# Placing the transposed maxima ahead of the parts' store on SyncE's queue

## The chip, the cores and the metric

The kernel runs on one core of one Trainium2 chip. The metric is the device time of one execution in microseconds (us); less is better. The core has TensorE (PE, matmuls), VectorE (DVE), ScalarE (ACT), GpSimd (POOL) and SyncE (SP), which here issues nearly all DMA transfers. Each engine runs its own program in order, and semaphores tie them together.

## The reference

Four layers on x of shape (32, 256, 128), each with a residual and a layer norm behind it: an attention with low-rank terms on q and v, a mixture of experts, a causal attention with rotary positions, and a routed spline network. What matters here is in the two attentions:

```
q, k, v = heads(x @ w_qkv)                 # 16 heads of 8, 256 positions, 32 sequences
att = softmax(q @ k.T * scale, axis=-1)    # second attention: causal
y = (att @ v).reshape(B, T, C) @ w_proj
x = layernorm(x + y)
```

## The kernel before

`attention` is built twice, as `attn0` and `attn1` (causal, rotary). One step of its pipeline takes in one sequence (a block); five steps lie between a block's load and its layer norm, and each engine runs `step` with the blocks at their lags: `st.has(2)` is the block that came in two steps ago. Three slots of `q_st` and `k_st` hold the stacks of three blocks. 5 steps are written out, then a loop runs three steps in a turn, then the rest is written out.

The scores need more than bf16, so GpSimd splits q and k of the entering block into three bf16 parts (L260 to L270, the last one counted by `lo_kept`). SyncE stores `parts` to a scratch in DRAM with two transfers (L218 and L220, counted by `parts_stored`) and one step later loads six stacks from it into `q_st` and `k_st` (L204): 72 rows a head, in which a single bf16 matmul sums the products of the parts.

The scores are made twice. `score_rows` (L523 is the causal mask, L527 the matmul) puts queries on the partitions; VectorE takes the row maxima (L346), splits them in two bf16 values (L357, L359, `mparts`), PE transposes these (L463) and ScalarE copies them to `mT_sb`, in two halves of 8 heads: half 0 with L331 at the twelfth of 16 score pairs of the step, half 1 with L302 early in the next step. A DMA of 8 KB, the placing, puts each half in two more rows of `q_st`: L225 for half 0, L193 for half 1. `score_cols` (L545 is the mask, L549 the matmul) then makes the scores again with keys on the partitions and the maximum already taken off; it waits for `m_placed[0]` at its first head of a step, for `m_placed[1]` at its ninth. ScalarE takes the exponential (L290), and PE sums the values (L566).

PE's step is written out by hand: 16 times a column score, a row score and whatever the table `AT` sets behind that pair, such as the transposition of x (L450), q and k (L471) and v (L493). SyncE's step has this order: the load of x for the next block (L184); wait for `mT_kept`, placing of half 1 (L193); wait for `parts_stored` and the six stack loads (L204); in `attn0` a load of `x_all` (L208); wait for `lo_kept` and for the scratch slot's former readers, and the two stores (L218, L220); wait for `mT_kept`, placing of half 0 (L225). GpSimd waits for `parts_stored` of the block before, before it writes `parts` again. ScalarE waits for the placing before it writes the same half of `mT_sb` again.

Of the kernel before, what the change touches and what calls it, by code (L numbers as in the profile page):

```python
# [26 lines left out]
KROWS = PARTS * PARTS * D  # L27
MROWS = 2
K_BLOCK = PARTS
STORES, STACKS = 2, PARTS  # L30
NH = H // 2
# [39 lines left out]
def apart(eng, mem):  # L71

    eng.sem_inc(mem["apart"], 1)


def wait(eng, sem, value):

    if not isinstance(value, int) or value > 0:
        eng.wait_ge(sem, value)


def pipeline(eng, step, slots=SLOTS, depth=DEPTH, total=B, ahead=1):


    first = depth
    loops = (total - ahead - first) // slots
    for s in range(first):
        step(Step(0, s, slots, total))
    with eng.Fori(0, loops) as i:
        for r in range(slots):  # L90
            step(Step(i, first + r, slots, total))
    for s in range(first + slots * loops, total + depth - 1):
        step(Step(0, s, slots, total))


def attention(nc, name, mem, causal, x_dram, lora, rope):
# [12 lines left out]
    with ExitStack() as ctx:  # L109
        def sb(label, shape, dt=F32):  # L110
            return ctx.enter_context(nc.sbuf_tensor(f"{name}_{label}", shape, dt))

        def sem(label):
            return nc.alloc_semaphore(name=f"{name}_{label}")

        scratch = nc.dram_tensor(f"{name}_scratch", (SLOTS, K_BLOCK + 2 * PARTS - 1, P, N), BF16, kind="Internal").ap()
        x_in, q_st, k_st, v_sb = (mem[k] for k in ("x_in", "q_st", "k_st", "v_sb"))
# [7 lines left out]
        mT_sb = sb("mT_sb", [MROWS * NH, 2, N], BF16)  # L125
# [25 lines left out]
        m_placed = [[sem(f"m_placed{g}{j}") for j in range(SLOTS)] for g in range(2)]  # L151
# [5 lines left out]
        xT_kept, qk_kept, v_kept, max_kept, mhi_kept, mparts_kept, mT_kept, probs_kept, oT_kept = (  # L157
            sem(x) for x in ("xT_kept", "qk_kept", "v_kept", "max_kept", "mhi_kept", "mparts_kept", "mT_kept",
                             "probs_kept", "oT_kept"))
# [17 lines left out]
        @block.sync  # L177
        def _(sp):
            def load_x(st, lag):

                wait(sp, xT_ready, st.seq(lag, c=1 - SLOTS))
                src = x_all[:, bass.ds(st.seq(lag, TB), TB), :] if x_dram is None else \
                    x_dram[:, bass.ds(st.seq(lag, TB), TB), :]
                sp.dma_start(x_in[:, st.slot(lag), :, :], src).then_inc(x_loaded[st.slot(lag)], 16)  # L184

            def step(st):
                if st.has(-1) and (x_dram is None or st.loop or st.off >= AHEAD - 1):
                    load_x(st, -1)
                if st.has(3):

                    sp.wait_ge(mT_kept, st.seq(3, 2, 2))
                    sl = st.slot(3)
                    sp.dma_start(q_st[KROWS:KROWS + MROWS, sl, NH:H, :], mT_sb[:, 1, :]).then_inc(m_placed[1][sl], 16)  # L193
                if st.has(1):
                    sl = st.slot(1)
                    sp.wait_ge(parts_stored[sl], st.turn(1, 16 * STORES))
                    apart(sp, mem)

                    wait(sp, cols_ready, st.seq(SLOTS + 1, H, H))

                    for j in range(PARTS):
                        rows = slice(PARTS * D * j, PARTS * D * (j + 1))
                        for stack, block, stacked in ((q_st, 0, q_stacked), (k_st, K_BLOCK + j, k_stacked)):
                            sp.dma_start(stack[rows, sl, :, :].rearrange("p h n -> p (h n)"),  # L204
                                         scratch[sl, block:block + PARTS].rearrange("a (d h) n -> (a d) (h n)", d=D))\
                                .then_inc(stacked[sl], 16)
                if st.has(2) and x_dram is not None:
                    sp.dma_start(x_all[:, bass.ds(st.seq(2, TB), TB), :],  # L208
                                 x_dram[:, bass.ds(st.seq(2, TB), TB), :]).then_inc(x_old_loaded[st.slot(2)], 16)
                if st.has(0):  # L210
                    sl = st.slot(0)
                    sp.wait_ge(lo_kept, st.seq(0, c=1))
                    apart(sp, mem)

                    wait(sp, q_stacked[sl], st.turn(SLOTS, 16 * STACKS))
                    apart(sp, mem)
                    wait(sp, k_stacked[sl], st.turn(SLOTS, 16 * STACKS))
                    sp.dma_start(scratch[sl, 0:2 * PARTS].rearrange("b p n -> p b n"),  # L218
                                 parts[:, :, :, :].rearrange("p s j n -> p (s j) n")).then_inc(parts_stored[sl], 16)
                    sp.dma_start(scratch[sl, 2 * PARTS:K_BLOCK + 2 * PARTS - 1].rearrange("b p n -> p b n"),  # L220
                                 parts[:, 1, 0:PARTS - 1, :]).then_inc(parts_stored[sl], 16)
                if st.has(2):
                    sp.wait_ge(mT_kept, st.seq(2, 2, 1))
                    sl = st.slot(2)
                    sp.dma_start(q_st[KROWS:KROWS + MROWS, sl, 0:NH, :], mT_sb[:, 0, :]).then_inc(m_placed[0][sl], 16)  # L225

            if x_dram is None:
                load_x(Step(0, 0, SLOTS, B), 0)
            pipeline(sp, step)

        @block.gpsimd
# [1595 lines left out]
```

## Time and profile before

| | us |
|---|---|
| median of 3 runs | 1456.69 (1455.31 to 1460.36) |
| profiled execution | 1455.56 |
| its span | 1453.8 |
| PE busy in the span | 1117.4 (77%) |
| DVE / ACT / POOL busy | 1095.9 / 841.6 / 540.3 |

The first attention lies at about 35 to 535 us of the span, the mixture of experts behind it, the second attention at about 606 to 1180, and the spline network takes the rest. A row of the views below names line, engine, operation and tiles; in a timeline the first number is the start in us from the start of the span, the second the duration, and a bracket at the end gives the time for which the engine was idle before and what ended it. Ends of matmuls are modelled.

### The profile page before, as it was taken

What the parts mean: (1) busy time and instruction counts of PE and PEld (TensorE: products, weight loads), DVE (VectorE), ACT (ScalarE), POOL (GpSimd) and SP (SyncE); (2) the same over time, 40 slices, a digit from 0 to 9 for tenths busy, and PEclk for the clock granted to TensorE, in tenths of its full rate; (3) what the DMA queues carried; (4) which work ended last, traced back from release to release, by engine and by line L of the source; (5) the groups of instructions that cost most, each with busy time, mean ns of one, the idle gap of its engine ahead of it and who ended that gap; (6) DMA issues with size and microseconds to landing.
All of it is one profiled execution on the core that took longest, in us unless ns stands there. A gap on an engine that the chain in (4) does not pass through costs nothing. (4 is left out here: it accounts for less than half of the span.)

```text
span 1453.8 us, 36143 instructions
## 1 busy us (share of the span) xinstructions
PE 1117.4 (77%) x11411; PEld 778.6 (54%) x11411; DVE 1095.9 (75%) x2949; ACT 841.6 (58%) x1840; POOL 540.3 (37%) x568
## 2 busy tenths in 40 slices
PE   2699999999999995139999999999999948103220
PEld 1466666666666653126777777777777724002120
DVE  4589999999999976526677676676776756898996
ACT  1277777777777763616666666666666635103554
POOL 5323233332332203154455444554444142003555
PEclk9899999999999998559999999999999978655555
DMA  1655556556465513044444444444444202000111
GB/s 45 151 124 134 137 120 140 126 128 140 116 138 133 116 29 122 11 120 103 115 114 113 108 115 105 116 115 104 119 103 115 67 16 101 0 0 0 30 36 51
DMA packets 122513, 137.26 MB, mean 94 GB/s; under 512 B 12560, under 2 KB 110160, under 8 KB 113232
## 3 DMA queue, kind: packets, MB, share of 16 engines
q1 hardware_dynamic: 121408, 136.45, 38.8%
q8 instruction: 34, 0.56, 0.2%
q14 instruction: 31, 0.25, 0.1%
q10 hardware_dynamic: 1040, 0.00, 0.0%
HBM read 85.03 MB, written 37.75 MB: 84 GB/s over the span
## 5 line engine op out<-in xcount | busy, mean ns | idle before, releaser
L346 DVE TENSOR_REDUCE attn_negmax<-attn_row_ps 128x2 f32<-128x512 f32 (+1 forms) x1024 | 606.5, 618 | 216.0 <-PE attn_row_ps L527 203.6
L290 ACT ACTIVATE attn_probs<-attn_col_ps 128x512 f32<-128x512 f32 (+1 forms) x1024 | 539.9, 547 | 238.0 <-PE attn_col_ps L549 221.3
L527 PE MATMUL attn_row_ps<-k_st,q_st 72*128 72x256 bf16 (+1 forms) x2048 | 368.0, 261 | 15.3 <-DMA k_st<-attn_scratch 13.9
L549 PE MATMUL attn_col_ps<-q_st,k_st 74*128 74x256 bf16 (+1 forms) x2048 | 368.7, 261 | 2.7 <-ACT attn_probs L290 1.0
L566 PE MATMUL attn_out_ps<-attn_probs,v_sb 128*32 128x256 f32 (+1 forms) x4096 | 247.3, 359 | 1.3 <-ACT attn_probs L290 1.3
L549 PEld LDWEIGHTS attn_col_ps<-q_st,k_st 74*128 74x128 bf16 x2048 | 179.4, 98 | 91.6 <-ACT attn_probs L290 32.3
L527 PEld LDWEIGHTS attn_row_ps<-k_st,q_st 72*128 72x128 bf16 x2048 | 201.1, 99 | 40.7 <-issue 15.3
L275 POOL TENSOR_TENSOR attn_rstd<-attn_var,minus_half 128x2 f32<-128x2 f32 x64 | 45.5, 711 | 384.2 <-DVE attn_var L410 384.2
L523 PE MATMUL attn_row_ps<-mask_qk,ident_h 128*128 128x256 bf16 x512 | 140.8, 275 | 18.4 <-DMA k_st<-attn_scratch 17.8
L566 PEld LDWEIGHTS attn_out_ps<-attn_probs,v_sb 128*32 128x32 f32 x4096 | 106.9, 109 | 86.2 <-issue 20.4
L545 PE MATMUL attn_col_ps<-mask_kq,ident_h 128*128 128x256 bf16 x512 | 141.5, 276 | 13.8 <-DMA q_st<-attn_mT_sb 11.6
L250 POOL TENSOR_TENSOR attn_q_half<-attn_q_half,sin 128x512 f32<-128x512 f32 x32 | 40.6, 1267 | 182.5 <-ACT attn_qk L317 182.5
L1516 POOL TENSOR_TENSOR ffn_rstd<-ffn_var,minus_half 128x8 f32<-128x8 f32 x19 | 31.9, 1680 | 167.7 <-DVE ffn_var L1538 167.7
L260 POOL TENSOR_SCALAR attn_parts<-attn_qk 128x512 bf16<-128x512 f32 x64 | 39.7, 620 | 124.5 <-ACT attn_qk L314 112.8
L471 PE MATMUL attn_in_ps<-attn_xT,wqk 128*128 128x256 f32 x256 | 79.5, 437 | 2.4 <-ACT attn_xT L296 2.4
L1460 PE MATMUL ffn_r_ps<-ffn_table_hm,ffn_ohT 128*128 128x193 bf16 x64 | 21.0, 361 | 74.4 <-ACT ffn_ohT L1472 74.4
L545 PEld LDWEIGHTS attn_col_ps<-mask_kq,ident_h 128*128 128x128 bf16 x512 | 49.5, 97 | 50.6 <-issue 18.3
L263 POOL TENSOR_TENSOR attn_rest<-attn_qk,attn_parts 128x512 f32<-128x512 f32 x64 | 74.1, 1157 | 5.3
L270 POOL TENSOR_TENSOR attn_parts<-attn_rest,attn_parts 128x512 bf16<-128x512 f32 x64 | 74.0, 1157 | 5.3
L1449 PE MATMUL ffn_o_ps<-ident_h,ffn_onehot 128*128 128x128 bf16 x64 | 10.1, 312 | 73.4 <-PEq L1164 73.4
L523 PEld LDWEIGHTS attn_row_ps<-mask_qk,ident_h 128*128 128x128 bf16 x512 | 49.3, 96 | 28.1 <-issue 18.5
L1479 ACT ACTIVATE ffn_z<-ffn_y,ffn_shift,ffn_rstd 128x128 f32<-128x128 f32 x64 | 26.4, 482 | 54.9 <-DVE ffn_shift L1543 54.9
(228 smaller groups left out, 1687.2 us busy)
## 6 DMA issues: line engine op xcount, KB each, us to landing
q_st<-attn_scratch SPq DMA_DIRECT2D x192, 192.0 KB
k_st<-attn_scratch SPq DMA_DIRECT2D x192, 192.0 KB
attn_scratch<-attn_parts SPq DMA_DIRECT2D x64, 384.0 KB, 3.0
attn_scratch<-attn_parts SPq DMA_DIRECT2D x64, 128.0 KB, 3.7
x_in<-in_L_attn_x_dram SPq DMA_DIRECT2D x32, 128.0 KB, 2.1
x_all<-in_L_attn_x_dram SPq DMA_DIRECT2D x32, 128.0 KB, 7.0
moe_xs<-x_all SPq DMA_DIRECT2D x8, 512.0 KB, 3.0
x_in<-x_mid SPq DMA_DIRECT2D x32, 128.0 KB, 2.1
```

The lines of the kernel that those rows point to most:

```text
L250: nc.gpsimd.tensor_tensor(q_half[:, :, :], q_half[:, :, :], sin, ALU.mult).then_inc(sin_done, 1)
L263: nc.gpsimd.tensor_tensor(rest[:, :, :], qk[:, :, :], parts[:, :, 0, :], ALU.subtract)\
L270: nc.gpsimd.tensor_tensor(parts[:, :, 2, :], rest[:, :, :], parts[:, :, 1, :], ALU.subtract)\
L275: nc.gpsimd.tensor_tensor(rstd[:, :], var[:, :], mem["minus_half"][:, 0:TB], ALU.pow)\
L290: nc.scalar.activation(probs[:, u % 2, j, 0:W], col_ps[:, n % 2, 0:W], ACT.Exp, scale=scale).then_inc(probs_kept, 1)
L346: nc.vector.tensor_reduce(negmax[:, t, 2 * p:2 * p + 2], row_ps[:, row_bank(st, u), 0:2 * keys].rearrange("p (a k) -> p a k", a=2), AX_X, ...
L471: last = nc.tensor.matmul(in_ps[:, s * N:(s + 1) * N], wqk[:, s, :], xT[:, st.slot(0), :], start=True, stop=True)
L523: nc.tensor.matmul(seen[:, :, keys - P:keys], ident_h[:, :], mask_qk[:, :, :], start=True, stop=False, skip_group_check=True)
L527: last = nc.tensor.matmul(bank[:, a * keys:(a + 1) * keys], q_st[0:KROWS, sl, h, t * P:(t + 1) * P], k_st[0:KROWS, sl, h, 0:keys], start=n ...
L545: nc.tensor.matmul(seen[:, :, 0:P], ident_h[:, :], mask_kq[:, :, :], start=True, stop=False, skip_group_check=True)
L549: last = nc.tensor.matmul(bank[:, t * N:(t + 1) * N - first], k_st[0:rows, sl, h, t * P:(t + 1) * P], q_st[0:rows, sl, h, first:N], start= ...
L566: last = nc.tensor.matmul(out_ps[32 * j:32 * j + 32, g * N + first:(g + 1) * N], v_sb[:, st.slot(lag), t, 32 * h:32 * h + 32], probs[:, u ...
```

## The change

In SyncE's step the wait for the first half of the transposed maxima and its placing stand ahead of the wait for the parts and their two stores, in place of behind them. Nothing else is changed; both attentions use this code.

```diff
@@ -207,6 +207,10 @@
                 if st.has(2) and x_dram is not None:
                     sp.dma_start(x_all[:, bass.ds(st.seq(2, TB), TB), :],
                                  x_dram[:, bass.ds(st.seq(2, TB), TB), :]).then_inc(x_old_loaded[st.slot(2)], 16)
+                if st.has(2):
+                    sp.wait_ge(mT_kept, st.seq(2, 2, 1))
+                    sl = st.slot(2)
+                    sp.dma_start(q_st[KROWS:KROWS + MROWS, sl, 0:NH, :], mT_sb[:, 0, :]).then_inc(m_placed[0][sl], 16)
                 if st.has(0):
                     sl = st.slot(0)
                     sp.wait_ge(lo_kept, st.seq(0, c=1))
@@ -219,10 +223,6 @@
                                  parts[:, :, :, :].rearrange("p s j n -> p (s j) n")).then_inc(parts_stored[sl], 16)
                     sp.dma_start(scratch[sl, 2 * PARTS:K_BLOCK + 2 * PARTS - 1].rearrange("b p n -> p b n"),
                                  parts[:, 1, 0:PARTS - 1, :]).then_inc(parts_stored[sl], 16)
-                if st.has(2):
-                    sp.wait_ge(mT_kept, st.seq(2, 2, 1))
-                    sl = st.slot(2)
-                    sp.dma_start(q_st[KROWS:KROWS + MROWS, sl, 0:NH, :], mT_sb[:, 0, :]).then_inc(m_placed[0][sl], 16)
```

## Rows read from the trace of the kernel before

**Rows 1.** Stretch of the second attention: busy time (x count) of each engine, granted clock, DMA.

```profile
640.00:1160.00 520.00, 503.17 (x5634) 374.56 (x5633) 363.10 (x1013) 334.33 (x759) 240.38 (x239) 0.99 0.46 108
```

**Rows 2.** Waits of PE, second attention: us in total, times, longest.

```profile
PE attn_col_ps L545 <- DMA q_st<-attn_mT_sb: 11.6, 23, 4.6
```

**Rows 3.** First attention: SP and ACT in a step; PE's waits, 35 to 535.

```profile
312.35 0.39 SPq L218 DMA_DIRECT2D attn_scratch<-attn_parts  x1
...
316.32 0.66 SPq L225 DMA_DIRECT2D q_st<-attn_mT_sb  x1
...
322.68 0.33 SPq L204 DMA_DIRECT2D q_st<-attn_scratch  x1
...
315.95 0.34 ACT L331 COPY attn_mT_sb<-attn_in_ps 16x256 bf16<-16x256 bf16 x1
...
PE attn_row_ps L527 <- DMA k_st<-attn_scratch: 13.9, 1, 13.9
...
PE attn_col_ps L549 <- DMA q_st<-attn_mT_sb: 0.4, 1, 0.4
```

**Rows 4.** Second attention, a steady step: timeline of ACT.

```profile
900.43 0.36 ACT L331 COPY attn_mT_sb<-attn_in_ps 16x256 bf16<-16x256 bf16 x1
```

**Rows 5.** The same step: timeline of SP, the DMA queue's own.

```profile
900.98 0.39 SPq L218 DMA_DIRECT2D attn_scratch<-attn_parts  x1
...
902.08 0.65 SPq L225 DMA_DIRECT2D q_st<-attn_mT_sb  x1
...
906.54 0.63 SPq L193 DMA_DIRECT2D q_st<-attn_mT_sb  x1
```

**Rows 6.** Timeline of PE around the scores that open a step.

```profile
887.68 0.28 PE L545 MATMUL attn_col_ps<-mask_kq,ident_h 128*128 128x256 bf16 x1 [0.32 <-ACT attn_probs L290]
...
903.74 0.38 PE L527 MATMUL attn_row_ps<-k_st,q_st 72*128 72x256 bf16 x2
...
904.40 0.28 PE L545 MATMUL attn_col_ps<-mask_kq,ident_h 128*128 128x256 bf16 x1 [0.28 <-DMA q_st<-attn_mT_sb]
...
920.32 0.38 PE L527 MATMUL attn_row_ps<-k_st,q_st 72*128 72x256 bf16 x2
...
1136.49 0.28 PE L545 MATMUL attn_col_ps<-mask_kq,ident_h 128*128 128x256 bf16 x1 [0.18 <-DMA q_st<-attn_mT_sb]
```

**Rows 7.** The drain of the second attention: SP, then PE.

```profile
1148.11 0.62 SPq L225 DMA_DIRECT2D q_st<-attn_mT_sb  x1
...
1151.24 0.27 PE L545 MATMUL attn_col_ps<-mask_kq,ident_h 128*128 128x256 bf16 x1
```

**Rows 8.** Start of the second attention: ACT, SP, PE, and the stretch 650 to 655.

```profile
646.54 0.36 ACT L331 COPY attn_mT_sb<-attn_in_ps 16x256 bf16<-16x256 bf16 x1 [5.37 <-PE attn_in_ps L463]
...
650.52 0.79 SPq L225 DMA_DIRECT2D q_st<-attn_mT_sb  x1
...
652.94 0.39 PE L545 MATMUL attn_col_ps<-mask_kq,ident_h 128*128 128x256 bf16 x1 [4.62 <-DMA q_st<-attn_mT_sb]
...
671.43 0.28 PE L545 MATMUL attn_col_ps<-mask_kq,ident_h 128*128 128x256 bf16 x1 [1.37 <-DMA q_st<-attn_mT_sb]
...
650.00:655.00 5.00, 2.06 (x12) 1.67 (x13) 0.42 (x1) 0.86 (x2) 0.00 (x0) 0.50 0.47 133
```

**Rows 9.** DVE's split and PE's transposition of the second half: steady step, then drain.

```profile
905.09 0.17 DVE L359 TENSOR_TENSOR attn_mparts<-attn_negmax,attn_mparts 128x16 bf16<-128x16 f32 x1
...
905.84 0.28 PE L463 MATMUL attn_fin_ps<-ident_h,attn_mparts 128*16 128x128 bf16 x2
...
1152.38 0.18 DVE L359 TENSOR_TENSOR attn_mparts<-attn_negmax,attn_mparts 128x16 bf16<-128x16 f32 x1
...
1152.70 0.27 PE L463 MATMUL attn_fin_ps<-ident_h,attn_mparts 128*16 128x128 bf16 x2 [0.18 <-DVE attn_mparts L359]
```

**Rows 10.** Stores: count, KB each, median us to landing; first, then second attention.

```profile
attn_scratch<-attn_parts SPq DMA_DIRECT2D x31, 384.0 KB, 5.5
...
attn_scratch<-attn_parts SPq DMA_DIRECT2D x30, 384.0 KB, 2.8
```

## The prediction

> **What bounds the kernel now.** I read the stages first. In the second attention TensorE (PE) is busy 503.17 of 520 us at granted clock 0.99, against 363 for VectorE, 334 for ScalarE and 240 for GpSimd [rows 1]: PE is the bound, so only a hole in PE's own row can give time back. Next, the waits. PE's one repeated wait for a DMA there is for `q_st<-attn_mT_sb`, the placing of the transposed maxima: 11.6 us in 23 waits [rows 2]. In the first attention the same wait is 0.4 us, once, and the wait for the stacks is the fill, once [rows 3]. Then one steady step of the second attention, engine by engine. ScalarE has the first half of the maxima (`mT_sb[:, 0]`, L331) ready at 900.43 + 0.36 = 900.79 [rows 4]. SyncE issues the store at 900.98, so the parts are ready at nearly the same time, and the placing only at 902.08 [rows 5]: it stands 1.29 us behind its data, because SP's program has the store, with its three waits and two issues, ahead of it. PE's next column score (L545, the first of the step) starts at 904.40 with a wait noted for that DMA [rows 6], 2.32 us after the issue.
>
> How large is the hole? The last row score before it (L527) starts at 903.74. In an undisturbed queue the next instruction starts 0.22 us after a 256-wide L527 pair; this one starts 0.66 after it, so the hole is 0.44 us. (The view's idle, 0.28, counts from a modelled end; it is 0.16 smaller.) From 904.40 to the last L527 of the next step, 920.32, plus 0.22, is 16.14 us of PE work without a hole [rows 6]. The step is 16.56.
>
> **The change, part by part.**
>
> *The placing moves ahead of the store, second attention.* It is then issued when its data is there. In the first attention SP waits there already, and its issue at 316.32 is 0.03 us behind the copy's end at 315.95 + 0.34 = 316.29 [rows 3]; I take 0.03. The placing comes 1.26 us earlier (1.29 - 0.03), the hole needs only 0.44, so 0.82 us is left over. That so long a distance ends the wait is seen in the drain, where no store stands ahead: placing issued at 1148.11, column score at 1151.24, 3.13 us later and without a wait noted [rows 7].
>
> The sum, over the column scores that open a step. From 671.43 to 1136.49 there are 28 steps, 465.06 us [rows 6, 8]. Their work is 28 x 16.14 = 451.9, and 8 of them have 16.28 (887.68 to 903.74, plus 0.22: one in three, the first step of a turn of the loop) [rows 6], which makes 453.0. The holes in between are 12.0 us. To this comes the hole that ends at 671.43: 1.37 idle, 1.53 by starts [rows 8]. The first placing of the stage is the largest: maxima at 646.54 + 0.36 = 646.90, issue at 650.52, since SP stood waiting for the parts, and PE idle 4.62 us up to 652.94 [rows 8]. There the landing stays the limit, so I count what the issue gains, 3.62 - 0.03 = 3.59. Together 3.59 + 1.53 + 12.04 = 17.16 us.
>
> *What is late next.* The second transposition of maxima (L463, after two more scores) waits for VectorE's L359. Now it starts at 905.84, 0.75 after L359 started at 905.09. L359 depends on row scores before the hole, so it does not move when PE does. In the drain L463 does wait for it, and starts 0.32 after L359 (1152.38, 1152.70) [rows 9]. So 0.43 us of slack is left against 0.44 of hole. Where the two nearly cancel I allow 0.02 us a step, 0.5 us in 28. Sum: 16.7 us. ScalarE and GpSimd work between 334 and 240 us in the 520 [rows 1], and shift along with PE.
>
> *The store goes behind the placing, second attention.* It costs the placing's 0.65 us of issue: store at about 901.65 in place of 900.98. It is read back only after the second placing, issued at 906.54 [rows 5]. Its second transfer, issued 0.44 after the first, lands in 2.8 us [rows 10], at 904.9. Cover 1.6 us, cost nothing. If the cover were gone, SP would issue the stack loads that much later.
>
> *The store goes behind the wait for the maxima, first attention.* Here the parts are ready early: store at 312.35, placing at 316.32. Behind SP's wait now stand both stores; behind them the load of `x_in`, which was behind this wait before. The store goes to about 317.2, 4.8 us later, its second transfer to 317.65. It lands in 2.8 us as in the second attention, or in 5.5 as now in the first [rows 10]: at 320.5 or 323.2. The stack loads were issued at 322.68 [rows 3]; by the one nothing moves, by the other they go 0.5 us later. I take the lower value: 5.5 is measured in the midst of the stack loads, and the new place is behind them. GpSimd's next splitting waits for the same landing, and has nothing to store before the next placing. Either way the stack is read a step after it is loaded. The placing in this attention keeps its time to 0.1 us, and PE, with no hole at it, gains nothing. Bounds of this part: 0 and, with no slack in the stacks, 29 x 0.5 = 14.5 us; below nothing if the loads, now without the store among them, let something start earlier, but PE waits for none of them, so no gain.
>
> *One term hangs on the clock.* From 650 to 655 the granted clock is 0.50, that is 1.2 GHz [rows 8]; PE was idle 4.62 us of it. If the clock rises as long after the restart as now, that stretch only moves. If the shorter hole lets it rise sooner, the matmuls at 1.2 GHz shrink by at most half of the 2.06 us that PE was busy in that window: 1.0 us more. The Trainium skill ("TensorE: Matmul & The Clock Gate", Part 1: The HAM clock gate) says that the clock follows how busy PE has been recently. By that rule the second case is open, sum 17.7; by the row it cannot be told, and I take 0.
>
> The landing is the other. The row has 2.32 us with the store 1.10 us ahead. The Trainium skill ("DMA: Bandwidth & Descriptors", Queues, rings and completion order) says that an engine consumes descriptors in ring order. By that the placing now stands behind the store's share and would land sooner when it is put ahead; no row here shows a placing with nothing ahead and someone waiting. By the row the first placing gains 3.59, by the rule a little more.
>
> **Where the time comes out.** The profiled execution took 1455.56 us (span 1453.8); the median of the three runs is 1456.69, 1.13 above. 1455.56 - 16.7 = 1438.9, and on the median's footing 1440.0.
>
> **Rivals.**
> - *Another wait takes the hole's place.* The hole before 887.68 is put down to ScalarE's exponential (L290), not to the DMA [rows 6], and L463 may need all of its 0.75 us. Then the 28 steps keep their length and only the start gives: 3.59 + 1.53 = 5.1, so 1451.6. Against the exponential: at 1151.24 the same kind of score starts with none noted, and by the code it needs only the exponential before the last. Against L463: its 0.32 in the drain.
> - *The start gives more.* Clock and landing in the first step together add up to 1.5 to 2.5: 1438.
> - *The change does not do what it says*: the landing is not counted from the issue but ends with the traffic around it, and PE's hole stays. 1456.7. Against: the wait ends 2.42 us after its issue in the first step (650.52, 652.94) and 2.32 after it in the steady one (902.08, 904.40), though the first stands 3.62 and the other 1.29 behind its data [rows 5, 6, 8].
> - *Slower*: in the first attention the late store holds the stack loads. It decides when the store lands over 5.0 us after its issue (322.68 - 317.65) and the stacks have no slack. At 6 us each of 29 steps is 1 us longer: 1440 + 29 = 1469. For it: 5.5 is on record. Against: PE's wait for the stacks is the fill alone [rows 3].
>
> **How the numbers follow.** Forecast 1440.0: 0.80. More at the start, 1438: 0.05. Another wait, 1451.6: 0.07. No effect, 1456.7: 0.04. Slower, 1469: 0.04. The range is 1436 to 1447: at its low end the start gives 2.5 and the median falls 1.5 below the profiled footing, at its high end L463 or the landing gives back 0.2 us in each of 28 steps (5.6) and the median 1.4. A measurement of this kernel can tell about 0.3%, 4.4 us. The rival of 5.1 us stands at this bound and is halved: faster 0.88, same 0.08, slower 0.04.
>
> **What would show it.** In the changed kernel the first of SP's stores in a step follows the placing by about 0.7 us, in both attentions. In the second the placing stands 0.03 behind L331's end, the wait for `q_st<-attn_mT_sb` is down to one of about 1 us, the step is 16.1 to 16.3 and the stage some 17 us shorter. If the hole stays at the opening score with another name beside it, the first rival holds. If waits for L359 at L463 are over 0.1 us each, my slack was too generous. If the first attention's step grows beyond 15.26, the store's landing is to blame. The prediction is wrong if the second attention's steps stay at 16.5.

## The result and the profile after

The changed kernel takes 1439.18 us (median of 4 runs, 1437.38 to 1442.32), the kernel before 1456.0 (1455.04 to 1460.36); the ratio is 0.9881, interval 0.9853 to 0.9909. The forecast was 1440.0, in a range of 1436 to 1447. Beside other runs it came again: 1440.2 us, ratio 0.9885 (0.9854 to 0.9917).

First the second attention as one stretch and its waits, to be read against [rows 1] and [rows 2]: busy time of PE, PE's weight loads, DVE, ACT and POOL, then granted clock, DMA share and GB/s; under it all the waits of PE for a DMA or an engine in that stretch.

```profile
640.00:1160.00 520.00, 515.65 (x5789) 389.47 (x5788) 371.64 (x1036) 343.54 (x780) 241.26 (x240) 0.98 0.46 109
...
PE attn_in_ps L493 <- ACT attn_qk L317: 1.7, 2, 0.9
PE attn_fin_ps L463 <- DVE attn_mparts L359: 1.0, 3, 0.6
PE attn_in_ps L463 <- DVE attn_mparts L359: 0.8, 1, 0.8
PE attn_col_ps L545 <- ACT attn_probs L290: 0.3, 1, 0.3
PE attn_col_ps L545 <- DMA q_st<-attn_mT_sb: 0.3, 1, 0.3
```

PE is busy 515.65 us of the same 520, 12.5 more than before. The wait for the placing went from 11.6 us in 23 to 0.3 in one, and no other name took its place in the steady steps: the three waits for L359 at L463 (0.18, 0.18 and 0.59 us) stand at 1124 and later, where the stage drains.

A steady step now, ACT, SP and PE, to be read against [rows 4], [rows 5] and [rows 6]:

```profile
893.13 0.36 ACT L331 COPY attn_mT_sb<-attn_in_ps 16x256 bf16<-16x256 bf16 x1
...
893.52 0.63 SPq L213 DMA_DIRECT2D q_st<-attn_mT_sb  x1
894.50 0.40 SPq L222 DMA_DIRECT2D attn_scratch<-attn_parts  x1
...
898.81 0.63 SPq L193 DMA_DIRECT2D q_st<-attn_mT_sb  x1
899.56 0.34 SPq L204 DMA_DIRECT2D q_st<-attn_scratch  x1
...
896.44 0.38 PE L527 MATMUL attn_row_ps<-k_st,q_st 72*128 72x256 bf16 x2
896.66 0.27 PE L545 MATMUL attn_col_ps<-mask_kq,ident_h 128*128 128x256 bf16 x1
...
912.59 0.38 PE L527 MATMUL attn_row_ps<-k_st,q_st 72*128 72x256 bf16 x2
912.81 0.27 PE L545 MATMUL attn_col_ps<-mask_kq,ident_h 128*128 128x256 bf16 x1
```

The placing (now L213) goes out 0.03 us after the copy's end (893.49) where it was 1.29 behind. PE's opening score follows the last row score by 0.22 us, with no bracket, where it was 0.66. The step is 16.15 us, where the same step took 16.56.

The start of the second attention, against [rows 8]:

```profile
651.00 0.36 ACT L331 COPY attn_mT_sb<-attn_in_ps 16x256 bf16<-16x256 bf16 x1 [6.92 <-PE attn_in_ps L463]
...
651.39 0.79 SPq L213 DMA_DIRECT2D q_st<-attn_mT_sb  x1
652.41 0.38 SPq L222 DMA_DIRECT2D attn_scratch<-attn_parts  x1
...
653.51 0.40 PE L545 MATMUL attn_col_ps<-mask_kq,ident_h 128*128 128x256 bf16 x1 [0.30 <-DMA q_st<-attn_mT_sb]
...
650.00:655.00 5.00, 4.11 (x23) 2.83 (x24) 4.07 (x11) 0.85 (x2) 1.98 (x3) 0.50 0.36 100
```

PE's idle time before the opening score fell from 4.62 to 0.30 us. The placing is used 2.12 us after its issue, where it took 2.42.

In this profiled execution (1442.32 us, the slowest of the four) the gain is 13.2 us. To see where, I cut both traces at PE's first row score of an attention and at the transposition of the last block's x (L450), and took the differences of the starts; in the second attention also at its first two L450:

| stretch, us | before | after | difference |
|---|---|---|---|
| first attention | 440.58 | 442.09 | +1.5 |
| its drain, the experts, the fill of the second | 148.77 | 150.27 | +1.5 |
| second attention | 484.79 | 468.68 | -16.1 |
| of it: to its first L450 | 18.14 | 15.81 | -2.3 |
| of it: first to second L450 | 18.07 | 16.31 | -1.8 |
| of it: the rest | 448.58 | 436.56 | -12.0 |
| behind it | 333.28 | 333.29 | 0.0 |

The 3 us lost outside are not shown to come from the order. Stretches one and two together take 589.35 us before, 592.36 after, 590.94 when the changed kernel is run again, and 591.02 in a kernel that has the old order in the first attention (the first experiment below). The granted clock names part of it in the first trace. It dips where the first attention drains, whichever kernel runs, but not by the same amount; the kernel before, then the one after:

```profile
520.00:530.00 10.00, 9.97 (x109) 6.83 (x108) 9.21 (x21) 6.80 (x15) 0.00 (x0) 1.00 0.05 14
530.00:540.00 10.00, 8.88 (x80) 4.36 (x80) 4.60 (x16) 6.46 (x13) 1.40 (x2) 0.83 0.01 3
```

```profile
520.00:530.00 10.00, 9.50 (x69) 5.75 (x70) 6.16 (x13) 4.36 (x9) 0.00 (x0) 0.66 0.06 16
530.00:540.00 10.00, 9.10 (x98) 5.09 (x96) 8.22 (x23) 7.32 (x16) 1.41 (x2) 1.00 0.01 3
```

The mean over the 20 us is 0.915 against 0.83, which is 1.7 us of full clock. The other half lies at the start of the first attention: not counting the one at its opening, the second L450 stands 29.73 us behind the first row score before and 31.17 after, and from there on the steps are alike (15.23 us on average in both).

### The profile page after: what moved, and what is told of

Read it like the earlier page. It is cut to its first block and busy times, and to the rows that moved or that the text cites. A ratio compares the mean times of both kernels' runs of the same rounds, so it can differ in the third digit from the quotient of the medians.

```text
span 1440.6 us, 36143 instructions
## 1 busy us (share of the span) xinstructions
PE 1118.2 (78%) x11411; PEld 784.9 (54%) x11411; DVE 1096.5 (76%) x2949; ACT 841.8 (58%) x1840; POOL 540.6 (38%) x568
## 5 line engine op out<-in xcount | busy, mean ns | idle before, releaser
L545 PEld LDWEIGHTS attn_col_ps<-mask_kq,ident_h 128*128 128x128 bf16 x512 | 49.5, 97 | 29.7 <-issue 18.2
```

What stands on the lines that cost most here:

```text
L545: nc.tensor.matmul(seen[:, :, 0:P], ident_h[:, :], mask_kq[:, :, :], start=True, stop=False, skip_group_check=True)
```

## The experiments

Times are medians; each ratio is to the kernel before, each diff against the changed kernel. "Stage" is the second attention as cut above.

**The change in the second attention alone.** The placing stands ahead of the stores where the attention is causal (the second), behind them where it is not.

```diff
-                if st.has(2):
+                if st.has(2) and causal:
                     sp.wait_ge(mT_kept, st.seq(2, 2, 1))
                     sl = st.slot(2)
                     sp.dma_start(q_st[KROWS:KROWS + MROWS, sl, 0:NH, :], mT_sb[:, 0, :]).then_inc(m_placed[0][sl], 16)
...
+                if st.has(2) and not causal:
+                    sp.wait_ge(mT_kept, st.seq(2, 2, 1))
+                    sl = st.slot(2)
+                    sp.dma_start(q_st[KROWS:KROWS + MROWS, sl, 0:NH, :], mT_sb[:, 0, :]).then_inc(m_placed[0][sl], 16)
```

> The placing goes ahead of the store in the second attention alone; the first attention keeps the order of before. My theory (the hole at the score that opens a step of the second attention is the issue delay of the placing): the whole gain is here, 16 to 17 us, ratio to before 0.988, steps of the second attention 16.15 to 16.2 us, those of the first 15.26. Rival (part of the gain comes from the first attention, where the stores move out of the stack loads): the gain is smaller than that of the full change by over 3 us.

1441.17 us, 0.9885 (0.9859 to 0.9911). The stage is 469.06 us, the wait for the placing 0.3 us once. The rival, over 3 us of the gain from the first attention, falls: the whole gain lies here, within what a run can tell.

**The change in the first attention alone.** The two conditions exchanged; the placing's lines are those of the diff above.

```diff
-                if st.has(2):
+                if st.has(2) and not causal:
...
+                if st.has(2) and causal:
+                    sp.wait_ge(mT_kept, st.seq(2, 2, 1))
...
```

> The placing goes ahead of the store in the first attention alone. My theory: no change, 1456 within 2 us; the first attention's steps stay at 15.26 us, its store goes out 4.8 us later, lands in under 3.5 us instead of 5.5, and the stack loads keep their time. Rival (the late store holds the stack loads and these have no slack): the steps of the first attention get longer, 0.5 us each, 14 us in all.

1456.82 us, 1.0001 (0.9987 to 1.0015): nothing. The steady steps of the first attention average 15.23 us, as before, where the rival would have made each 0.5 longer. The DMA view of the first attention (count, KB, median us to landing) has, for this kernel:

```profile
attn_scratch<-attn_parts SPq DMA_DIRECT2D x31, 384.0 KB, 2.8
attn_scratch<-attn_parts SPq DMA_DIRECT2D x31, 128.0 KB, 3.0
```

The store lands in 2.8 us in place of 5.5 [rows 10], since it no longer goes out in the midst of the stack loads. Of the two ends of the bound, 2.8 and 5.5, the lower was right.

**The placing between the two stores.** It goes behind the store of 384 KB and ahead of that of 128 KB.

```diff
-                if st.has(2):
-                    sp.wait_ge(mT_kept, st.seq(2, 2, 1))
-                    sl = st.slot(2)
-                    sp.dma_start(q_st[KROWS:KROWS + MROWS, sl, 0:NH, :], mT_sb[:, 0, :]).then_inc(m_placed[0][sl], 16)
                 if st.has(0):
...
                     sp.dma_start(scratch[sl, 0:2 * PARTS].rearrange("b p n -> p b n"),
                                  parts[:, :, :, :].rearrange("p s j n -> p (s j) n")).then_inc(parts_stored[sl], 16)
+                if st.has(2):
+                    sp.wait_ge(mT_kept, st.seq(2, 2, 1))
+                    sl = st.slot(2)
+                    sp.dma_start(q_st[KROWS:KROWS + MROWS, sl, 0:NH, :], mT_sb[:, 0, :]).then_inc(m_placed[0][sl], 16)
+                if st.has(0):
+                    sl = st.slot(0)
                     sp.dma_start(scratch[sl, 2 * PARTS:K_BLOCK + 2 * PARTS - 1].rearrange("b p n -> p b n"),
                                  parts[:, 1, 0:PARTS - 1, :]).then_inc(parts_stored[sl], 16)
```

> The placing stands between the two stores, behind the large one (384 KB) and ahead of the small one. My theory (only the issue time counts, with 0.82 us to spare): the placing is issued 0.65 to 0.75 us behind its data, the steady steps have no hole or one under 0.1 us, steps 16.15 to 16.25; the first step of the second attention stays nearly as before (its placing waits for the parts), so 3 us of the gain are lost: 1442 to 1443. Rival (the placing lands with the traffic of the store that stands ahead of it): the wait at the opening score stays at 0.3 us and more and the steps at 16.5, time 1451 to 1456.

1445.2 us, 0.9917 (0.9889 to 0.9945); 2 to 3 us above what I expected. The stage is 472.27 us, 3.6 more than in the first trace of the full change and 4.6 more than in its second (467.70, below). Up to the second L450 it takes 35.23 us against 32.12 and 31.26, so the start loses 3.1 to 4.0; the rest takes 437.04 against 436.56 and 436.44, since one step in three has 16.24 to 16.29 us where the full change has 16.20 or 16.21. SP and PE in a steady step, then at the start:

```profile
782.46 0.39 SPq L218 DMA_DIRECT2D attn_scratch<-attn_parts  x1
782.97 0.63 SPq L223 DMA_DIRECT2D q_st<-attn_mT_sb  x1
...
785.29 0.38 PE L529 MATMUL attn_row_ps<-k_st,q_st 72*128 72x256 bf16 x2
785.52 0.28 PE L547 MATMUL attn_col_ps<-mask_kq,ident_h 128*128 128x256 bf16 x1
...
651.73 0.79 SPq L223 DMA_DIRECT2D q_st<-attn_mT_sb  x1
...
654.27 0.40 PE L547 MATMUL attn_col_ps<-mask_kq,ident_h 128*128 128x256 bf16 x1 [3.90 <-DMA q_st<-attn_mT_sb]
```

Steady placings are 0.47 to 0.69 us behind their data, with 384 KB queued just ahead. PE's opening score stands 0.21 to 0.26 us behind the last row score, so no hole is over 0.04 us, and from the sixth block on none is over 0.01. Some placings are used 2.47 us after their issue without a hole. At the start an idle time of 3.90 stays. The rival, that the landing is tied to the store's traffic, would have kept the hole; it falls.

**All waits first, then the placing, then both stores.** SyncE takes the two waits of the stores (parts made, scratch slot free) ahead of the placing.

```diff
-                if st.has(2):
-                    sp.wait_ge(mT_kept, st.seq(2, 2, 1))
-                    sl = st.slot(2)
-                    sp.dma_start(q_st[KROWS:KROWS + MROWS, sl, 0:NH, :], mT_sb[:, 0, :]).then_inc(m_placed[0][sl], 16)
                 if st.has(0):
...
                     wait(sp, k_stacked[sl], st.turn(SLOTS, 16 * STACKS))
+                    apart(sp, mem)
+                if st.has(2):
+                    sp.wait_ge(mT_kept, st.seq(2, 2, 1))
+                    sl = st.slot(2)
+                    sp.dma_start(q_st[KROWS:KROWS + MROWS, sl, 0:NH, :], mT_sb[:, 0, :]).then_inc(m_placed[0][sl], 16)
+                if st.has(0):
+                    sl = st.slot(0)
                     sp.dma_start(scratch[sl, 0:2 * PARTS].rearrange("b p n -> p b n"),
                                  parts[:, :, :, :].rearrange("p s j n -> p (s j) n")).then_inc(parts_stored[sl], 16)
```

> SyncE first waits for the parts and for the scratch slot, then for the maxima, then issues the placing and behind it both stores: nothing stands ahead of the placing on the queue, but the wait for the parts does. My theory: the placing is 0.25 us behind its data in the steady steps, no hole, steps 16.15 to 16.2; the first step of the second attention gets back 0.8 us in place of 2.3 to 3.6, the second step nothing of its 1.5 is lost beyond 0.6: 1441 to 1443. The difference to the full change is the start alone, 2 to 3.5 us. Rival (the wait for the parts itself makes the hole): steps stay at 16.5.

1441.47 us, 0.9895 (0.9871 to 0.9918). Placings are 0.11 to 0.33 us late in the steady steps, steps 16.14 to 16.21. The rival, that the wait for the parts makes the hole, would have kept them at 16.5; it falls. The start keeps 2.86 us of idle time:

```profile
649.67 0.77 SPq L222 DMA_DIRECT2D q_st<-attn_mT_sb  x1
...
651.79 0.40 PE L548 MATMUL attn_col_ps<-mask_kq,ident_h 128*128 128x256 bf16 x1 [2.86 <-DMA q_st<-attn_mT_sb]
```

The stage is 470.33 us, 1.7 above the first trace of the full change and 2.6 above its second, where I gave 2 to 3.5. By time alone this kernel can't be told from the full change; by the traces the difference is the start (33.90 us up to the second L450, against 32.12 and 31.26; the rest is 436.43).

**The changed kernel again**, beside the three that follow.

> The changed kernel once more, beside the runs that follow. My theory: 1439 within 2 us, ratio 0.988; the second attention's steady steps 16.14 to 16.21. The opening of the second attention differs from execution to execution with the clock, by about 1 to 1.5 us. Rival (the gain of the first measurement was in part a matter of the chip): ratio above 0.991.

1440.2 us, as given above. The stage is 467.70 us, its steady part 436.44, 0.1 from the first trace; its first two pieces take 31.26 us together, against 32.12 in the first trace and 36.21 before. The start is what varies. The rival, a ratio above 0.991, falls with 0.9885.

**The change for the first two blocks alone.**

```diff
-                if st.has(2):
+                if st.has(2) and not st.loop and st.off < 4:
...
+                if st.has(2) and (st.loop or st.off >= 4):
+                    sp.wait_ge(mT_kept, st.seq(2, 2, 1))
...
```

> The placing goes ahead of the store only for the first two blocks of each attention; all later steps keep the order of before. My theory: what the start gives alone is 2.3 to 3.6 us at the first block and 1.5 to 1.8 at the second, together 4 to 5 us, so 1451 to 1452.5, ratio 0.9965 to 0.9975; steady steps stay at 16.5 to 16.75 with holes of 0.4. Rival (a later wait eats the start's gain): ratio 0.999 to 1.001.

1451.72 us, 0.996 (0.9944 to 0.9976): 4.5 us by the medians. The first two pieces take 31.22 us in place of 36.21, a gain of 5.0; the rest 448.63 us, as before (448.58). The two parts of the sum stand apart, and they add: 5.0 and 12.0. The rival, that a later wait eats the gain of the start, falls.

**The stores held back further**, until PE has made the third column score of the next step.

```diff
                     sp.dma_start(q_st[KROWS:KROWS + MROWS, sl, 0:NH, :], mT_sb[:, 0, :]).then_inc(m_placed[0][sl], 16)
+                if st.has(0) and st.has(3):
+                    sp.wait_ge(cols_ready, st.seq(3, H, 19))
+                    apart(sp, mem)
                 if st.has(0):
                     sl = st.slot(0)
```

> The changed order, and both stores held back until PE has made the third column score of the next step. In the second attention they then go out some 3.3 us behind the opening score, and the stack loads start at 6.8 behind it in place of 3.0; in the first attention the store goes out 1.8 behind it and the loads 5.2 in place of 3.6. My theory (the late store is covered, since the stack loads take 8 us and are not read before the next step opens, 16.2 or 15.3 us after the score): no change to the full change, 1439 to 1441. Rival (the late store is the danger of this change and the stacks have no slack): 1 to 4 us a step in either attention, over 1470.

1450.6 us (1445.01 to 1454.11), 0.996 (0.9942 to 0.9977). Theory and rival were both wrong: it costs some 10 us against the full change, and hardly by the stacks coming late. In the profiled execution the first attention takes 449.00 us, 7 more than after the full change, and the second 470.70, 2 to 3 more. PE's wait for the placing is back in the first attention. It waits for a stack in the fills, and else only twice, 0.88 us at 1129.55 and 0.49 at 1144.67, at the end of the second attention. Waits of PE, then SP, PE and stretches of one step of the first attention:

```profile
PE attn_col_ps L552 <- DMA q_st<-attn_mT_sb: 7.6, 20, 1.1
...
346.16 0.32 SPq L204 DMA_DIRECT2D q_st<-attn_scratch  x1
...
353.10 0.65 SPq L213 DMA_DIRECT2D q_st<-attn_mT_sb  x1
...
356.31 0.39 PE L552 MATMUL attn_col_ps<-q_st,k_st 74*128 74x256 bf16 x2 [0.37 <-DMA q_st<-attn_mT_sb]
...
353.00:354.00 1.00, 1.00 (x10) 0.93 (x10) 1.00 (x3) 1.00 (x3) 0.00 (x0) 1.00 0.78 156
354.00:355.00 1.00, 1.00 (x18) 0.51 (x17) 0.97 (x4) 0.64 (x2) 0.00 (x0) 1.00 0.62 106
355.00:356.00 1.00, 0.94 (x12) 0.31 (x4) 0.96 (x6) 0.25 (x1) 0.00 (x0) 1.00 0.24 42
```

The held store starts the stack loads 5.4 us behind the opening score in place of 3.7. These loads, with the load of `x_all` that is issued behind them at 348.74, are then still running when the next placing goes out (DMA share 0.78 of 16 engines; in the changed kernel it is 0.01 there, from 348 to 349 with the placing at 348.14). The placing is used after 3.21 us, where 2.67 passed in the changed kernel without a wait. The stacks themselves are in time.

**Held until the sixth column score.** The same edit with 22 in place of 19.

> As the run before, held until the sixth column score of the next step: store 7 us behind the opening score in the second attention, loads at 10.7, landing near 18.6, and the second placing of the step behind the store too, landing near 10.5 where PE asks for it at 8.8. My theory: the cover ends between the two runs; the second attention's steps grow by 1.5 to 2.5 us and the first's by 1 to 3, 1500 to 1560 in all. Rival (there is far more slack than I think, or the transfers are faster when spread): under 1460.

1735.29 us, 1.1909 (1.186 to 1.1958). The direction was right, the size was not: steps of 20.8 us in the first attention and 20.5 in the second, 5.6 and 4.3 us more than in the changed kernel. The waits of PE from 100 to 500 us, in the first attention, and that stretch in this kernel and in the changed one:

```profile
PE attn_col_ps L552 <- DMA q_st<-attn_mT_sb: 60.5, 36, 2.7
PE attn_fin_ps L466 <- DVE attn_mparts L362: 0.2, 1, 0.2
...
100.00:500.00 400.00, 338.93 (x2903) 211.98 (x2901) 276.95 (x635) 220.10 (x442) 95.22 (x116) 0.87 0.42 94
```

```profile
100.00:500.00 400.00, 392.52 (x3996) 262.89 (x3994) 366.72 (x869) 291.63 (x604) 129.60 (x157) 1.00 0.57 130
```

PE waits nearly twice a step (36 waits in some 19 steps) and all but once for placings: the first half's lands late behind the stack loads, the second half's is issued behind the held stores. The waits are 3.1 us a step. The other half is the clock: PE is busy some 17.6 us a step in place of 14.9, at a granted clock of 0.87 in place of 1.00. That the waits bring the clock down fits these rows and is not shown by itself; nor have I taken apart how the two delays feed each other through the hold, which itself follows PE.

## Why the prediction was right

Point by point, by its own steps.

**The total.** 1440.0 forecast, 1439.18 measured; in the stage, 16.7 forecast, 16.1 and 17.1 measured in the two traces of the changed kernel. The mechanism is shown below, but so close a total has some luck in it: the start gave 0.1 to 1.0 us less than its term, and the steady steps 0.8 to 0.9 more.

**The bound and the hole.** Right. The hole at the opening score was the issue delay of the placing. Four positions of the placing show it: 0.03, 0.11 to 0.33 and 0.47 to 0.69 us behind its data give no hole to speak of (0.04 at most), 1.1 to 1.3 (before) gives 0.3 to 0.5. The slack of 0.82 us that the sum had left over was there: in the steady steps the placing now stands 3.06 to 3.14 us ahead of its use.

**The steady term.** 12.04 us forecast less 0.5 given back, over the 28 steps between the opening scores at 671.43 and 1136.49. Between the same two scores the changed kernel takes 452.70 us (670.25 to 1122.95) and 452.59 when run again, where before took 465.06: 12.4 and 12.5 us. (The 12.0 of the table covers 27 steps.) The holes were read rightly; the surplus is in the work. Two steps in three take 16.14 to 16.16 us, the third 16.20 or 16.21, where I had 16.28. Those 0.07 us lay between the opening column score and the next one (0.80 us, now 0.73). Why they were there stays open: the kernel with the placing between the stores still has them (0.79), with a hole of 0.01 us at most ahead of them.

**What is late next.** L359 did stay where it was when PE moved: 0.69 us behind the opening score before (905.09 and 904.40), 1.13 now. Where PE now asks, DVE and PE stand like this, against [rows 9]; the last line, of the kernel before, is PE's row score ahead of the L463 that [rows 9] shows at 905.84:

```profile
897.79 0.17 DVE L359 TENSOR_TENSOR attn_mparts<-attn_negmax,attn_mparts 128x16 bf16<-128x16 f32 x1
...
897.77 0.38 PE L527 MATMUL attn_row_ps<-k_st,q_st 72*128 72x256 bf16 x2
898.11 0.27 PE L463 MATMUL attn_fin_ps<-ident_h,attn_mparts 128*16 128x128 bf16 x2
```

```profile
905.52 0.38 PE L527 MATMUL attn_row_ps<-k_st,q_st 72*128 72x256 bf16 x2
```

L463 stands 0.32 us behind L359, as where it waited for it in the drain. No bracket is noted, but it stands 0.34 behind its row score in 20 of the 28 steps (0.33 to 0.35), where it was 0.31 or 0.32 before; in the other eight it is 0.31 still. So the two just meet, and L463 comes some 0.02 us late in two steps of three: the allowance of 0.02 a step had the right size, and the step as a whole grew by 0.01 to 0.02. More time taken from PE ahead of L463 should show as a wait there (not tried). The next limit of this step is named.

**The start.** Mechanism right, size off. The first placing stands 0.03 us behind its data in place of 3.62, but the opening shortened by 2.3 in this trace. PE worked through the row scores ahead of it at 1.2 GHz, which before had run in part at the full clock, and was ready itself only 0.3 us before the landing (one wait of 0.3 where I had one of about 1). The stretches, before and then after:

```profile
640.00:645.00 5.00, 3.60 (x28) 2.16 (x27) 3.66 (x10) 1.15 (x3) 3.53 (x3) 0.97 0.70 147
645.00:650.00 5.00, 2.53 (x17) 1.33 (x17) 4.41 (x11) 0.36 (x1) 3.77 (x5) 0.71 0.01 3
```

```profile
640.00:645.00 5.00, 4.12 (x16) 2.87 (x15) 1.81 (x3) 1.86 (x5) 0.77 (x1) 0.50 0.71 159
645.00:650.00 5.00, 4.80 (x26) 2.92 (x25) 3.97 (x9) 0.00 (x0) 4.55 (x5) 0.50 0.38 77
```

In the repetition (granted clock 0.90 and 0.78 in these stretches) and in the run with the start alone (1.00 and 0.64) the opening took 14.35 and 14.33 us, a gain of 3.8. The second piece gave 1.8 and 1.2 where I had 1.53. Together 4.1 to 5.0, forecast 5.12. The two cases on the clock that I had left open looked at the wrong place, behind the landing; what counted was the clock ahead of it, and that differs from one execution of the same kernel to the next. I had also misread a row there: of the 4.62 us of idle time only 2.94 lie in the stretch from 650 to 655, the rest before it.

**The landing.** Where PE waits for it, it is 2.42 us at the start and 2.30 to 2.57 in later steps with both stores ahead, 2.54 with the large one ahead, and 2.12 with nothing ahead (the full change, and the run with all waits first). The ring order of the Trainium skill ("DMA: Bandwidth & Descriptors", Queues, rings and completion order), by which an engine takes descriptors in the order of its ring, has the right sign: ahead of the stores the first placing lands 0.3 us sooner, 2.12 in place of 2.42. That counts only at the start.

**The stores behind the placing.** Nothing, as forecast, in both attentions. In the steady steps the first store follows the placing by 0.8 to 1.0 us where I had 0.7. In the first attention the second transfer goes out at 334.32 in the changed kernel, lands 3.0 us later at 337.3, and the stack loads start at 339.07: 1.7 us of cover. I had placed the danger, in a landing of over 5.0 us, at the stacks. The held stores show that it lies elsewhere: well before the stacks come late their loads run into the next placing (by the first held run; the share of `x_all` in it was not taken apart). So the slower rival had a true cover and a wrong mechanism.

**The other rivals.** ScalarE's exponential beside the hole at 887.68 was a coincidence of times: before, PE has six waits for it from 640 to 1160 (1.8 us), and with the placing early one of 0.3 us is left. That the change does not do what it says is excluded by the between run, which has the store ahead and no hole.

**Open.** Why the first attention and what follows it up to the second vary by 3 us between profiled executions. The clock's dip there is no sufficient cause: in the six traces of the first six experiments it is 0.83 over 520 to 530 us and 1.00 behind it, as much as the kernel before loses 10 us later, and the two stretches still total from 589.1 to 591.3 us among them. Nor is the order the cause: the kernels with the old order in the first attention show 589.58 (start alone) and 591.02, those with a new one 589.11 (all waits first) and 590.94 (after again). Some 2 us of it arise in the first 32 us of the first attention: the L450 named above stands 29.3 to 29.7 us behind the first row score in three kernels (before, all waits first, start alone) and 31.2 to 32.2 in the other five, of which the second and third experiment have a granted clock of 1.00 all through it. The start-alone kernel has the same order there as the changed one.

## What to carry to other kernels

A queue that issues in program order makes every transfer wait for the waits of those ahead of it. Where a small transfer is needed at once and a large one is not needed for microseconds, measure for each the distance from its data to its issue and from its landing to its use, and put the one without cover first. A hole in the bound engine is worth its length only, not the delay that made it: of 1.26 us won at the issue, 0.44 came back. Before moving a transfer later, look not only at who reads it but at what its followers will then overlap: here the loads behind the store reached the next placing first.

## What the runs showed of the hardware

An 8 KB transfer from SBUF to SBUF, issued by SyncE, was used by PE 2.12 us after its issue with nothing just ahead of it on the queue (2.10 to 2.13 over seven kernels, first block of the second attention), 2.30 to 2.57 us with stores of 384 or 512 KB issued 0.4 to 1.1 us earlier, and 3.21 us in the midst of loads that kept the DMA engines 0.6 to 0.8 busy. A 384 KB store took 2.8 us to land away from such loads and 5.5 in their midst (medians). A wait of 0.3 us that is put down to an engine can be a coincidence: six steps of the kernel before, one in three in the middle of the stage, name ScalarE for a hole that went when the DMA came early. The idle time in the view is shorter than the hole, since it counts from a modelled end: 0.28 against 0.44 us at 904.40.
